# Earlier release of held result scatters, a third PSUM bank for late expert tiles, and a reordered attention tail

## What is computed

```python
x = x + attn_a(layernorm(x))      # 16 heads of 64, 256 x 256 scores with a relative bias
x = x + ffn(layernorm(x))         # 8 experts, each token goes through one
x = x + attn_b(layernorm(x))      # 64 x 32 tokens with a latent for keys and values, causal
x = x + ffn(layernorm(x))         # the same experts' weights again
# ffn: e = argmax(softmax(x @ Wr + br)); gate = its probability
#      y = (relu(xn @ W1[e] + b1[e]) @ W2[e] + b2[e]) * gate
```

## Time and profile before

| | us |
|---|---|
| median of 3 runs | 679.28 (679.26 to 679.71) |
| the profiled execution | 679.71 |
| its span, first to last instruction | 678.3 |
| PE busy | 649.6 (96%) |
| DVE, ACT, POOL busy | 478.9, 534.2, 365.1 |
| mean granted TensorE clock | 0.991 |

### The profile page before, as it was taken

The page is one execution under the profiler, slowest core; times in us unless marked ns, Lnnn a source line. Parts: engine busy times, 40 slices in busy tenths (PEclk is TensorE's granted clock), DMA queues, the critical chain, the costliest instruction groups (busy, mean ns, idle before and its releaser), DMA issues.

```text
span 678.3 us, 17768 instructions
## 1 busy us (share of the span) xinstructions
PE 649.6 (96%) x5406; PEld 548.4 (81%) x5406; DVE 478.9 (71%) x2155; ACT 534.2 (79%) x1776; POOL 365.1 (54%) x678
## 2 busy tenths in 40 slices
PE   6999999999999999989997999999999999989996
PEld 5778887878888888779885788888888888868996
DVE  4876767776777777978643767687868777796843
ACT  3997888887888978766753998898989898985663
POOL 4653545474556554716372455464755575562537
PEclk9999999999999999999997999999999999999999
DMA  8999989999100000035412000000000000022140
GB/s 267 281 285 294 284 215 316 296 269 285 49 5 15 17 1 7 28 95 166 126 40 57 2 2 1 2 2 9 17 10 2 10 24 3 17 61 67 51 113 20
DMA packets 67468, 64.65 MB, mean 95 GB/s; under 512 B 7793, under 2 KB 63998, under 8 KB 67120
## 3 DMA queue, kind: packets, MB, share of 16 engines
q1 hardware_dynamic: 62624, 56.41, 30.8%
q0 software_dynamic: 3136, 6.34, 2.8%
q10 hardware_dynamic: 1616, 0.79, 0.4%
HBM read 19.93 MB, written 44.75 MB: 95 GB/s over the span
## 4 chain that ended last, share of the span: by engine, by line
PE 82%; DVE 8%; issue 3%; DMA 2%; POOL 2%; ACT 2%; SPq 0%; DVEq 0%; POOLq 0%; ACTq 0%
PE ps L468 16%; PE ps L614 15%; PE ps L577 14%; PE ps L463 10%; PE ps L464 8%; PE ps L465 8%; PE ps L717 4%; PE ps L731 4%; DVE ring L1213 2%; PE ps L651 1%; DMA xs_scratch<-row,posi 1%; DMA wkn<-in_w_qkv 1%; PE ps L669 1%; DMA f_xs<-xs_scratch 1%; POOL ring L351 1%
## 5 line engine op out<-in xcount | busy, mean ns | idle before, releaser
L351 POOL TENSOR_SCALAR ring<-ring,rs 128x256 f32<-128x256 f32 (+1 forms) x500 | 219.4, 456 | 213.8 <-DVE rs L1224 213.0
L916 ACT ACTIVATE ring<-ring,mn 128x256 f32<-128x256 f32 (+1 forms) x512 | 243.3, 488 | 0.0
L468 PE MATMUL ps<-ident,ring 128*128 128x128 f32 x896 | 121.4, 275 | 3.7 <-POOL ring L351 3.2
L577 PE MATMUL ps<-qk 64*128 64x256 f32 (+1 forms) x1024 | 115.2, 363 | 0.9 <-DVE mn L1213 0.6
L614 PE MATMUL ps<-pt,v 128*64 128x256 f32 (+1 forms) x1024 | 112.3, 361 | 0.4 <-DVE pt L1242 0.3
L468 PEld LDWEIGHTS ps<-ident,ring 128*128 128x128 f32 x896 | 102.4, 143 | 10.1 <-POOL ring L351 4.3
L916 ACT ACTIVATION_READ_ACCUMULATOR ring<-ring,mn 128x1 f32 x512 | 104.0, 203 | 0.0
L614 PEld LDWEIGHTS ps<-pt,v 128*64 128x64 f32 x1024 | 66.3, 137 | 44.8 <-issue 15.3
L577 PEld LDWEIGHTS ps<-qk 64*128 64x128 f32 x1024 | 82.6, 187 | 18.8 <-issue 9.3
L884 ACT COPY qk<-ps 128x512 f32<-128x512 f32 x128 | 74.9, 585 | 24.6 <-PE ps L465 23.6
L1213 DVE CUSTOM_DVE_ANT_0 ring<-ps,cm 128x128 f32<-128x128 f32 (+1 forms) x256 | 73.9, 351 | 6.0 <-PE ps L577 5.6
(11 more groups left out here) (212 smaller groups left out, 1350.2 us busy)
## 6 DMA issues: line engine op xcount, KB each, us to landing
xs_scratch<-padt SPq DMA_DIRECT2D x16, 2064.0 KB, 22.2
f_xs<-xs_scratch SPq DMA_DIRECT2D x50, 129.0 KB, 2.3
w<-in_W SPq DMA_DIRECT2D x16, 256.0 KB, 6.1
xs_scratch<-padt SPq DMA_DIRECT2D x2, 1677.0 KB, 22.2
T<-in_bias SPq DMA_DIRECT2D x2, 512.0 KB, 7.8
T<-in_bias SPq DMA_DIRECT2D x1, 1024.0 KB, 10.3
bu<-in_w_kv_up SPq DMA_DIRECT2D x1, 1024.0 KB, 6.8
row<-in_x SPq DMA_DIRECT2D x1, 768.0 KB, 12.3
```

The costliest lines, as they stand in the source:

```text
L351: i = pool.tensor_scalar(ring[:, hh, it, 0:w], ring[:, hh, it, 0:w], rs[:, q], 1.0, ALU.mult, ALU.mult)
L468: return pe.transpose(out, src, ident[:, :])
L577: i = pe.matmul(PS[u % 2][hh][:, 256 * it:256 * it + w], qk[rows, 128 * it:128 * it + 128], qk[rows, 256:256 + w], start=True, stop=True)
L916: i = act.activation(ring[:, hh, it, 0:w], ring[:, hh, it, 0:w], ACT.Exp, bias=mn[:, q], scale=-1.0, accum_out=sm[:, q])
```

## The change

- `back`: the hold on POOL waits for the loads of groups 3 to 5 (tiles 12 to 19) instead of 3 to 6.
- `INDEX_LATE`, `INDEX_TR`: parts 5 and 6 of the index one step earlier each (74 and 75). Part 2 goes from step 63, after `TR(59)`, to step 62, after the steps of `post_a2`.
- `h_bank`: tile 22 uses bank 1, so that tiles 20, 21 and 22 have a bank each. Tile 24 then waits for the relu of tile 20 instead of that of 22. `Y(22)` comes after `H(24)` instead of before.
- ACT: the high part `keep(60)` goes from step 66 (after `relu(0)`) to step 65, before the copy of `XT(0)`.
- DVE: in step 63 `weigh(61)` and `TR(60)` come between the minima `S(62)` and `S(63)`. Before, `weigh(61)` was after `S(63)`, and `TR(60)` at the head of step 64.

```diff
-INDEX_TR = {60: 0, 63: 2}
-INDEX_LATE = {75: 5, 76: 6}
+INDEX_TR = {60: 0, 62: 2}
+INDEX_LATE = {74: 5, 75: 6}
             if n == HOLD:
-                for g in range(GROUP_OF[F_EACH], GROUP_OF[NF - 1]):
+                for g in range(GROUP_OF[F_EACH], GROUP_OF[F_MORE]):
                     pool.wait_ge(d_xs[g], 16 * (GROUPS[g][1] - GROUPS[g][0]) * (st + 1))
     def h_bank(n):
-        return ps[1 + n % 2] if n < 16 else ps[4 + n % 2]
+        return ps[1 + n % 2] if n < 16 else ps[1] if n == NF - 3 else ps[4 + n % 2]
             if n < 16:
                 claim(1 + n % 2, a_fr, NF * st + n + 1)
+            elif n == NF - 3:
+                claim(1, a_fr, NF * st + n + 1)
             else:
-                pe.wait_ge(a_fr, NF * st + n - 1)
+                pe.wait_ge(a_fr, NF * st + n - (3 if n == NF - 1 else 1))
...
-            if n == NF - 1:
-                Y(n - 2)
             if 0 < n < NF:
                 H(n)
...
-            elif 2 <= n < NF + 2 and n not in (*AT_ONCE, F_MORE, F_MORE + 1, NF - 1):
+            elif 2 <= n < NF + 2 and n not in (*AT_ONCE, F_MORE, F_MORE + 1):
                 Y(n - 2)
...
-            if s % 2 == 0 and 6 <= s < LAST_KEEP:
+            if s % 2 == 0 and 6 <= s <= NU:
                 keep(s - 6)
...
             if n == 0:
+                keep(NU - 4)
                 XT(0)
...
-            if s == NU:
-                TR(s - 4)
...
-            if s in INDEX_TR:
-                index(INDEX_TR[s])
...
             if s < NU and (b := post_at(s, "a")) is not None:
                 post_a2(b)
+            if s in INDEX_TR:
+                index(INDEX_TR[s])
...
-                if s == NU - 3:
+                if s in (NU - 3, NU - 1):
                     weigh(s - 2)
+                if s == NU - 1:
+                    TR(NU - 4)
                 S(s)
-            if s % 2 and 3 <= s < NU and s != NU - 3:
+            if s % 2 and 3 <= s < NU and s not in (NU - 3, NU - 1):
                 weigh(s - 2)
```

## The result

The changed kernel takes 677.03 us (median of 6 runs, 676.57 to 678.12). The kernel before, run beside it, takes 679.6 (6 runs, 679.26 to 680.7). The ratio is 0.9961, interval 0.9948 to 0.9974: faster by about 2.6 us, where 4.5 were forecast. Against the 679.28 that the forecast started from, this ratio gives 676.6: inside the range of 672.0 to 677.0, close to its upper end, and above the 674.8 of the forecast. The profiled execution took 676.67, its span is 675.3.

What follows compares the result with a forecast made beforehand. PE carries 82% of the chain; POOL's scatter backlog sets the end and the restart. Terms -2.8 - 2.4 + 0.9 + 0.1 - 0.3 = -4.5 took 679.28 to 674.8 us, range 672.0 to 677.0.

Steps and rivals of the forecast that it cites:

- rival (b): Early release of POOL's scatters half lost because scatters and loads share the DMA engines: 677.4 us; chance 0.08.
- The hold in stage 0: POOL's scatters of tiles 6 to 19 start 2.76 earlier and PE's restart moves with them: -2.8 us, bounds -2.2 to -4.4.
- Stage 1's end: Earlier scatters and the third bank end the kernel at 675.9 against 678.3: -2.4 us, bounds -1.8 and -3.0.
- the share of the bank: At stage 1's end, without the third bank the term would be -1.8 instead of -2.4 us.
- The restart's clock: PE's low clock at the start of stage 1, hardly prevented by a shorter gap: -0.3 us, bounds +0.5 and -1.8.
- The copy of unit 60: PE's waits of 0.88 and 1.09 before `out_last` of step 66, for the low part of `keep(60)`, go.
- DVE's reordering: In the attention tail `TR(61)` on DVE comes later, costing 0.6 us in stage 0 and 0.55 in stage 1.
- a wait of about 2.3 before `PV(61)`: Sign of being right: in the attention tail PE waits this long on DVE's copy, with low clock behind it.
- The clock in the tails: PE's clock falls in both attention tails, costing 1.2 us each; stage 1 already pays about 0.6.
- The moves of the index parts: Parts 5 and 6 one step earlier on DVE: nothing, bounds -0.3 to +0.3; part 2's exchange covered by 1.0.

Runs made afterwards that it cites:

- e8: The changed kernel with DVE's old order at the attention's end and the hold only for tiles up to 15: 684.05 us, ratio 0.9866 to the kernel before.
- e11: The changed kernel with DVE's old order at the attention's end and the hold for tile 12 alone: 671.35 us, ratio 0.9874 to the kernel before.
- e9: The changed kernel with DVE's old order at the attention's end and without the third bank: 674.02 us against 680.06 for the kernel before, ratio 0.9904.
- e10: The changed kernel with DVE's old order at the attention's end, run on the third chip: 671.92 us, ratio 0.988 to the kernel before.
- e5: The kernel before with the third bank alone: 693.15 us against 692.74, ratio 1.0013.
- e7: The kernel before with only the high part of unit 60 ahead of `XT(0)` on ACT: 690.42 us against 692.74, ratio 0.9962.
- e4: The changed kernel as it is, run again on another chip: 690.93 us, ratio 0.999 to the kernel before.
- e3: The changed kernel with `weigh(61)` and `TR(60)` back in their old places on DVE: 685.69 us, ratio 0.9907 to the kernel before.
- e2: The kernel before with the attention tail's edits alone (index part, DVE's order, copy of unit 60 on ACT): 694.43 us, ratio 1.0033.
- e6: The changed kernel with the logits product `post_c(6)` writing to PSUM bank 1: 690.22 us, ratio 0.996 to the kernel before.
- e1: The kernel before with the shorter hold alone, in both stages: 686.04 us against 691.21, ratio 0.9908.
- e12: The changed kernel with DVE's old order at the attention's end and 10 result buffers instead of 11: 672.54 us, ratio 0.9895 to the kernel before.

## Why the prediction was right, and which of its terms was wrong

The sign and most of the mechanism were right, the size wasn't: 4.5 us were forecast and 2.6 measured. That this is still inside the range is in part luck. The range reached up to 677.0 for the sake of rival (b), a half lost release, which didn't come; a costlier reordering filled the same room.

**The hold in stage 0: right.** Forecast -2.8, measured -2.68. The landing was 0.4 slower than assumed, and scatters 6 to 19 took 0.26 less. The clause that scatters wouldn't disturb the loads held as well: rival (b) wanted a longer list than 17.52, and it is 17.26. e8 and e11 overlap scatters and loads far more, and don't lose by it. (In stage 1 the prediction's own rows give 3.76 earlier for tile 6, not 3.74.)

**Stage 1's end: right, 0.5 too large.** -1.93 against -2.4, inside the bounds. Tile 6's scatter came 0.6 later than assumed, but that isn't the reason: POOL had caught up and waited for the results of tiles 21 and 22. The results themselves were on time: counted from `XT(3)`, that of tile 22 was forecast at 26.1 and came at 26.08. What was mis-sized is the step from a result to its scatter. I took 0.3, the gap between two scatters of a full list; where POOL really waits it is 0.80, and the last two scatters follow that one. For the share of the bank, 0.6, the profiles of e9 and e10 speak. That it is nothing under the long hold isn't shown: e5 gave nothing, but without the backlog that was to explain it.

**The restart's clock: small, as said.** -0.69 against -0.3 in this profile, in its bounds. The low stretch behind it is 3.41 us long instead of 6.83. In e10 it is 6.83 again and the piece 7.97, so this term differs from run to run.

**The copy of unit 60: right.** 0.88 + 1.09 = 2.0 forecast, 2.3 measured alone (e7), in whose profile the wait is gone.

**DVE's reordering: the term that was too small, and partly for a wrong reason.** In the forecast's balance it had 0.6 + 0.55 for the later `TR(61)`, and 1.2 + 1.2 - 0.6 for the clock: 2.95. It measures 5.2 by the medians of e4 and e3, 5.7 by their ratios. Two other pairs, each from two comparisons and so less firm, agree by their ratios: 5.5 from the changed kernel and e10, 4.9 from e2 and e7. I followed `TR(60)`, the minima and `TR(61)` through DVE's list, but of the minima's other effect, that they free a PSUM bank, I said nothing; I gave PE "`TR(61)` and `PV(60)` are done sooner". They were done later, behind the logits product. The sentence "a wait of about 2.3 before `PV(61)`" is wrong in its place: 2.16 and 1.82, before `post_c(6)`. The length came out alike because both are one delay of DVE. And since the transposes of unit 61 now stood behind it, DVE's `TR(61)` came at 295.23, 9.65 after S(62); the forecast's 292.7 is 8.84 after it.

Of the 5.2, the profiles of after and e10 show 3.4 in the tails, those of e4 and e3 3.8. The rest is not seen in a profile. It fits that the changed kernel's runs had a mean granted clock of 0.988 to 0.993, and those of e10 0.993 to 0.996: a mean lower by 0.004 is 5 us more at half clock, which can cost up to 2.5. But where those stretches lie in runs without a trace isn't shown. The profiled run of the changed kernel had the best clock of its six (0.993), which may be why its pieces come so close to the forecast; the run as a whole was only 0.36 under the median, since it had lost 1.7 before the first mark.

**The clock in the tails: half right.** A fall was taken in both. In stage 0 it came, and it came in every profile with the new order and in none with the old, so there it belongs to the reordering. In stage 1 it didn't come. e4 has the same pattern with a fall of twice the length in stage 0; e2 and e6 have a fall in both. The Trainium skill ("TensorE: Matmul & The Clock Gate", section on the HAM clock gate) has the rate fall after an idle window. The trace doesn't agree: both falls in a tail, here and in the kernel before, came after stretches in which PE had worked 1.24 of 3.40 and 1.80 of 3.30.

The sum, by the runs: the reordering +5.2, the copy -2.3, hold and bank with the restart -5.8 (e10's -8.1 less the copy), together -2.9; measured -2.6. The forecast had +2.95, -2.0 and -5.5. The three terms come from three comparisons, and on the chip of e1 to e4 they don't add up as well: there the changed kernel is only 0.3 under the kernel before.

The moves of the index parts were not tried by themselves. e3 and e10 have them all, so whatever they cost is inside the numbers above.

## What to carry to other kernels

When work is moved on one engine, list for each thing it passes not only what that thing makes but also what it frees: here four minima freed a PSUM bank, and PE's whole list stood behind it. Don't put an operation that waits for another engine ahead of one that is ready and that this other engine waits for. A serial list of 1.29 us steps that ends behind everybody else is best shortened by starting it earlier: here the start was held for loads that lost nothing by it. Once a list has caught up with what feeds it, price the hand-over between the engines (0.80 here) and not the gap inside the list (0.3).

## What the runs showed of the hardware

Chips differ by more than this change. The kernel before takes 679 to 680 us in the first comparison and in that of e9 to e12, and 691 and 693 on the two chips between. The profiles put it in a few places. In each of e1 to e8, and in neither before, after nor e9 to e12, DVE waits one to four times before one of the results 12 to 17, mostly for 3 to 8 us, for something that the trace calls remote, and the scatters behind come late (in e3 the trace has such a wait in stage 1 alone). Scatters 6 to 19 then take 20.2 us instead of 17.5 in stage 0 (e3 against e10), and scatters 19 to 24 take 10.9 instead of 7.2. Timeline of DVE, stage 1 of e1:

```profile
661.39 0.29 DVE L1385 TENSOR_TENSOR f_ys<-ps,w 128x128 f32<-128x128 f32 x1 [4.28 <-remote]
...
665.73 0.29 DVE L1385 TENSOR_TENSOR f_ys<-ps,w 128x128 f32<-128x128 f32 x1 [3.66 <-remote]
```

The statistics of the new x start 2.24 after the issue of its load in e10, where DVE waits for it, and 4.5 after in e3, where DVE has no idle time ahead of them: on that chip late results and not the load set the restart. What those chips wait for stays open. In the code a result from tile 11 on waits for the landing of the scatter 11 tiles before; e12, meant to test that, ran on a chip without these waits.

The way to S(62) of stage 0, with the same instructions on PE in all kernels, took 283.24 to 285.58 us. That is as much as the change is worth, so pieces of two traces are to be compared from a mark behind it.
